# A hand-built first stage with its loops written out: magnitudes from scaled exponentials, tables in two halves, another drain order, and V's scale found earlier

## The chip, the cores and the metric

One core of a Trainium2 chip runs one program on five engines that go their own ways and meet at semaphores: PE (TensorE, matmuls), DVE (VectorE), ACT (ScalarE), POOL (GpSimd) and SP (SyncE, which here only issues DMAs). The metric is the device time of one execution in microseconds; less is better.

## The reference, cut to what matters

```
def _s4d_kernel(log_dt, C, B, inv_A_real, A_imag, L):        # H=128 heads, N=64 modes, L=1024
    dt = jnp.exp(log_dt)
    A = -jnp.exp(inv_A_real) + 1j * A_imag
    dtA = A * dt[:, None]
    Cc = Bc[None, :, :] * (C[..., 0] + 1j * C[..., 1])
    Cc = Cc * (jnp.exp(dtA) - 1.0) / A
    V = jnp.exp(dtA[:, :, None] * ell)                        # ell = 0..1023
    return 2.0 * jnp.einsum('chn,hnl->chl', Cc, V).real       # C is the input x, (16, 128, 64, 2)

h = _L0_tok_ref(...)                                          # the call above
h = h + _L0_attn_ref(_layernorm(h), Wq, bq, Wk, bk, Wv, bv, Wo, bo)      # 32 heads, causal
h = h + _L0_ffn_ref(_layernorm(h), gate, up, down: 4-bit levels plus low-rank parts, silu)
```

Only the first line of `h` and the layer norm behind it belong to the stage that is changed. Attention and the feed-forward part are the same in both kernels.

## The kernel before, in words

The program is one first stage, `ssm_and_norm`, a barrier, and then `layer` with everything else. The first stage makes `h` (written to `h0_tokens`) and its layer norm, split into two 16-bit parts `x_hi` and `x_lo` for the matmuls behind it. It works on all five engines at once.

**The front.** A power exp(dtA·l) is split over l = 128·i + 16·j1 + j0, so three short tables (8 + 8 + 16 = 32 entries for each head, 128 heads: 128 partitions by 4096) give all powers by products. The partitions are the 64 modes twice, for real and imaginary part. DVE makes dt and A (L305 to L318), then the phases (L324 to L332), which ACT turns into sines (L259 to L263). POOL makes the exponents of the magnitudes (L197) and ACT takes the exponential of all 4096 in one instruction (L253). DVE makes the coefficient of each mode by some fifty small operations on 128x128 (L333 to L384). Then the tables are multiplied by the magnitudes, `tab2` on POOL (L200) and `tab1` on DVE (L387), and DVE turns the coefficients into `a1` and `a2` (L391 to L397).

**The units.** Heads are taken 8 at a time, 16 units. For each unit:

- POOL makes the first half of `v` (L208) and the factors `w` (L211, L214), DVE the rest of `w` (L405), the second half of `v` (L407, into `v_second`) and their sum (L410);
- PE multiplies, `product` (L228, 16 fp32 matmuls that stand as 32 in the trace), ACT copies the result out, `columns` (L269, tile `n_xt`);
- PE transposes it, `to_tokens` (L235), ACT copies that out, `tokens` (L279, `n_tok`), and SP writes it to DRAM (L185);
- DVE takes mean and variance (L414 to L417), ACT the root (L273), DVE the inverse (L421, L422), ACT normalises (L283);
- PE transposes back, `to_features` (L242), ACT writes the high part (L287), DVE the low part (L426).

Every engine runs a fixed order of these steps, written by hand with a lag in units for each step. In visit k PE does `to_features(k-5)`, `product(k-1)`, `to_tokens(k-2)`; ACT does `columns(k-2)`, the root of k-4, `tokens(k-3)`, `normalise(k-4)`, `high(k-5)`; DVE does the inverse of k-4, the factors of k, the mean of k-3, `low(k-5)`. Visits in the middle are turns of a hardware loop (`Fori`) with two units each, the first three and the last three pairs are written out. Most tiles have two buffers, `n_pt`, `n_pn` and `v_second` have one.

**V's scale.** While this runs, the first group of V's weights is in SBUF (`wv_raw`). Its largest value over all partitions sets a power of two: `find_big` on DVE (L530), `exchange` by two DMAs through DRAM on SP (L517, L519), `find_scale` on DVE (L536 to L540), then `first.high` on ACT (L545) and `first.low` on DVE (L550) split it. `find_big` and `find_scale` stand in the last visits of DVE, the exchange behind SP's loop.

Of the kernel before, what the change touches and what calls it, by code (L numbers as in the profile page):

```python
# [11 lines left out]
ALU = mybir.AluOpType  # L12
# [3 lines left out]
P = 128  # L16
# [65 lines left out]
LAG = 6  # L82


def ssm_and_norm(nc, ssm, cr, ci, h0_dram, xn_hi, xn_lo, ident, w_first, wv_first, b_first, first, rooms):
# [9 lines left out]
    with ExitStack() as st:  # L95
        sb = rooms.filler("v2", "small")

        def sem(name):
# [50 lines left out]
        def channels(n, s, start=0, end=UH):  # L149
            return bass.ds((n * 2 + s) * UH + start, end - start)  # L150

        def run(eng, stages, chain=None, marks=0, tail=lambda n: None):

            def iterations(n, known):
                for b in two:
                    for lag, work in stages:
                        d = b - lag
                        if not known or 0 <= 2 * n + d < UNITS:
                            work(n + d // 2, d % 2)

            for n in range(LAG // 2):
                iterations(n, True)
            before = chain.count if chain else 0
            with eng.Fori(0, VIS - LAG // 2) as n:
                if chain:
                    chain.loop(n, marks)
                iterations(n + LAG // 2, False)
            if chain:
                chain.end(VIS - LAG // 2, marks, before)
            for n in range(VIS, VIS + LAG // 2):  # L170
                iterations(n, True)
                tail(n - VIS)

        @block.sync
        def _(sp):
            sp.dma_start(par[:], ssm).then_inc(s_in, 16)
            sp.dma_start(cre[:], cr).then_inc(s_c, 16)
            sp.dma_start(cim[:], ci).then_inc(s_c, 16)
            sp.dma_start(first.bias[:], b_first).then_inc(first.s_bias, 16)
            sp.dma_start(first.raw_v[:], wv_first).then_inc(first.s_raw_v, 16)  # L180
            sp.dma_start(first.raw[:], w_first).then_inc(first.s_raw, 16)
            with sp.Fori(0, VIS) as n:
                for s in two:
                    sp.wait_ge(s_tok[s], n + 2)
                    sp.dma_start(h0_dram[:, channels(n, s), :], tok[s][:]).then_inc(s_out[s], 16)  # L185
            first.exchange(sp, 0)
            for s in two:
                sp.wait_ge(s_out[s], 16 * VIS + 16)

        @block.gpsimd  # L190
        def _(pool):
# [9 lines left out]
            pool.wait_ge(s_tab2, 1)  # L201
            pool.wait_ge(s_tab1, 1)
            pool.wait_ge(s_c, 32)

            def factors(n, s):

                pool.wait_ge(s_mm[s], n + 1)
                nc.gpsimd.tensor_tensor(four(v[s], TJ), bc(tab1[:, channels(n, s), TI:2 * TI], TJ, 3),  # L208
                                        bc(tab1[:, channels(n, s), 2 * TI:TAB], TI, 2), ALU.mult).then_inc(s_v1[s], 1)
                pool.wait_ge(s_a, 2)  # L210
                nc.gpsimd.tensor_tensor(four(w[s][0], C), bc(a1[:, channels(n, s), :], C, 3),  # L211
                                        bc(cre[:, channels(n, s), :], KT, 2), ALU.mult)
# [1647 lines left out]
```

## Time and profile before

| | us |
|---|---|
| median of 3 runs | 2087.96 |
| lowest, highest | 2087.77, 2090.44 |
| the profiled execution, time | 2088.66 |
| the profiled execution, span | 2086.7 |

The span runs from the first to the last instruction. PE is busy for 1896.5 us of it (91%), DVE for 1163.6 (56%), ACT for 612.7 (29%), POOL for 618.0 (30%). The chain of work that ended last is PE's for 73% of the span, DVE's for 8%. In forty slices of the span PE is busy for nine tenths or more from the eleventh slice to the end; in the first four slices (52 us each) it is busy for 0, 3, 7 and 7 tenths, and DVE for 8, 9, 9 and 8. The granted clock of PE is printed beside the busy times of a stretch as a share of its full 2.4 GHz; its other level is 1.2 GHz.

A row of the timeline is: start, duration (both us), engine, line, operation, tile written <- tiles read, shapes; in brackets how long the engine had been idle, and who ended that. Rows of a line give in ns the least, the median and the greatest duration, then the first and last start in us. SPq is SP's queue of DMA issues.

### The profile page before, as it was taken

Reading aid. Unit: us, or ns where it says so; the run is one execution under the profiler, and the core shown is the slowest. Engines: PE = TensorE matmul, PEld = TensorE weight load, DVE = VectorE, ACT = ScalarE, POOL = GpSimd, SP = SyncE. Lnnn points to the kernel's source line nnn. Section 1 sums busy time; section 2 is a strip of 40 time slices with the busy share of each in tenths; the row PEclk is TensorE's granted clock in tenths of the full one; section 3 lists DMA queues with packets and bytes.
Section 4 is the critical chain, followed back from the end, with each engine's and each line's share of the span. In section 5 each row is a group of like instructions: output and inputs, shape, how many; then the busy total and the mean of one; then the engine's idle time right before and its main releaser. Section 6 shows DMA issues by size and latency. Waiting matters only on the chain.

```text
span 2086.7 us, 31307 instructions
## 1 busy us (share of the span) xinstructions
PE 1896.5 (91%) x13212; PEld 1029.0 (49%) x13212; DVE 1163.6 (56%) x1476; ACT 612.7 (29%) x869; POOL 618.0 (30%) x261
## 2 busy tenths in 40 slices
PE   0377699999999898878999999999999999999999
PEld 0367576666656554444554444444444444444444
DVE  8998547777777778855644544444444444210111
ACT  2154324334333334421112333333333333200000
POOL 2675013343333334433310322232232232011101
PEclk9998799999999999999999999999999999999999
DMA  2022211111132112135441321322322232533441
GB/s 90 10 71 60 65 35 33 39 39 35 29 94 72 27 36 60 57 104 194 154 147 61 119 94 62 101 91 61 101 91 77 85 101 72 195 120 116 142 142 41
DMA packets 99812, 173.32 MB, mean 83 GB/s; under 512 B 13984, under 2 KB 75168, under 8 KB 91744
## 3 DMA queue, kind: packets, MB, share of 16 engines
q1 hardware_dynamic: 99680, 171.41, 25.7%
q8 instruction: 102, 1.67, 0.3%
q14 instruction: 30, 0.25, 0.0%
HBM read 114.22 MB, written 56.11 MB: 82 GB/s over the span
## 4 chain that ended last, share of the span: by engine, by line
PE 73%; DVE 8%; POOL 2%; issue 2%; ACT 2%; DMA 1%; SPq 1%; ACTq 0%; DVEq 0%
PE acc L1194 14%; PE acc L1123 14%; PE acc L1124 14%; PE ps_p L930 3%; PE ps_p L931 3%; PE ps_p L932 3%; PE acc L1044 3%; PE acc L1045 3%; PE acc L1046 3%; PE ps_t L957 2%; PE ps_p L946 2%; PE ps_p L948 2%; PE ps_p L947 2%; DVE prob L1464 2%; PE ps_l L1139 2%
## 5 line engine op out<-in xcount | busy, mean ns | idle before, releaser
L1123 PE MATMUL acc<-x_hi,q_f 128*128 128x512 f16 x1376 | 522.0, 379 | 0.0
L1124 PE MATMUL acc<-x_lo,q_f 128*128 128x512 f16 x1376 | 521.5, 379 | 0.0
L1194 PE MATMUL acc<-down_levels,hid_parts 128*128 128x512 f16 x1376 | 300.1, 379 | 0.0
L890 POOL TENSOR_TENSOR prob<-prob,mx 128x1024 f32<-128x1024 f32 x64 | 121.4, 1897 | 421.9 <-DVE mx L1471 421.9
L1123 PEld LDWEIGHTS acc<-x_hi,q_f 128*128 128x128 f16 x1376 | 134.5, 98 | 174.8 <-issue 17.8
L899 POOL TENSOR_SCALAR q_f<-q_raw 128x2048 f16<-128x2048 int32 x22 | 121.1, 5504 | 316.3 <-PE acc L1124 315.4
L1194 PEld LDWEIGHTS acc<-down_levels,hid_parts 128*128 128x128 f16 x1376 | 133.2, 98 | 163.1 <-issue 5.0
L1124 PEld LDWEIGHTS acc<-x_lo,q_f 128*128 128x128 f16 x1376 | 134.7, 98 | 156.9
L930 PE MATMUL ps_p<-x_hi,w_qk 128*128 128x512 f16 x512 | 196.8, 384 | 0.0
L931 PE MATMUL ps_p<-x_lo,w_qk 128*128 128x512 f16 x512 | 196.0, 383 | 0.0
L932 PE MATMUL ps_p<-x_hi,w_qk 128*128 128x512 f16 x512 | 195.7, 382 | 0.0
L1749 DVE TENSOR_TENSOR y<-acc,down_scale 128x1024 f32<-128x1024 f32 (+1 forms) x17 | 19.8, 1162 | 252.3 <-PE acc L1194 252.3
L228 PE MATMUL ssm_ps<-phase,magnitude 128*128 128x128 f32 x512 | 73.7, 313 | 87.9 <-DVE magnitude L410 87.9
L1699 DVE SCALAR_TENSOR_TENSOR up<-acc,gu_scale,low_term 128x512 f32<-128x512 f32 x84 | 63.0, 750 | 154.7 <-PE acc L1124 154.7
L946 PE MATMUL ps_p<-w_v,x_hi 128*128 128x256 f16 x512 | 140.6, 275 | 9.0 <-PEq L674 8.8
L948 PE MATMUL ps_p<-w_v,x_lo 128*128 128x256 f16 x512 | 140.6, 275 | 0.0
L947 PE MATMUL ps_p<-w_v,x_hi 128*128 128x256 f16 x512 | 140.6, 275 | 0.0
L1375 ACT ACTIVATE low_term<-ps_l,g_b_back 128x512 f32<-128x512 f32 x168 | 106.0, 682 | 115.6 <-PE ps_l L1139 115.6
L1392 ACT ACTIVATE hidden<-up 128x512 f16<-128x512 f32 (+1 forms) x88 | 55.4, 629 | 287.3 <-DVE up L1708 287.3
L893 POOL TENSOR_TENSOR prob<-prob,sm 128x1024 f32<-128x1024 f32 x64 | 120.4, 1897 | 57.0 <-DVE sm L1478 57.0
L1689 DVE SCALAR_TENSOR_TENSOR gate<-acc,gu_scale,low_term 128x512 f32<-128x512 f32 x84 | 63.0, 751 | 117.9 <-ACT low_term L1375 117.9
L1253 ACT ACTIVATE pth<-ps_t 128x512 f16<-128x512 f32 x128 | 76.0, 594 | 161.0 <-PE ps_t L957 161.0
(284 smaller groups left out, 3081.5 us busy)
## 6 DMA issues: line engine op xcount, KB each, us to landing
q_raw<-in_gu_q SPq DMA_DIRECT2D x22, 1024.0 KB, 7.1
hidden_parts<-hidden SPq DMA_DIRECT2D x42, 512.0 KB, 3.5
hid_parts<-hidden_parts SPq DMA_DIRECT2D x15, 1376.0 KB, 6.7
down_raw<-in_down_q SPq DMA_DIRECT2D x22, 512.0 KB, 5.1
w_raw<-in_w_qk SPq DMA_DIRECT2D x8, 1024.0 KB, 4.8
h_tokens<-n_tok SPq DMA_DIRECT2D x16, 512.0 KB, 3.8
o_parts<-ot SPq DMA_DIRECT2D x32, 256.0 KB, 2.3
wv_raw<-in_w_o SPq DMA_DIRECT2D x8, 1024.0 KB, 4.8
```

The costliest lines, as they stand in the source:

```text
L890: nc.gpsimd.tensor_tensor(prob[s % 2][p][:], prob[s % 2][p][:], bc(mx[p][:], H, 2), ALU.subtract).then_inc(s_sub[p], 1)
L893: nc.gpsimd.tensor_tensor(prob[s % 2][p][:], prob[s % 2][p][:], bc(sm[p][:], H, 2), ALU.mult).then_inc(s_prob[p], 1)
L899: nc.gpsimd.tensor_scalar(q16[i % 2][:], qraw[:], Q_ZERO, None, ALU.subtract).then_inc(s_q, 1)
L930: nc.tensor.matmul(out[:], w[:, j % 2, m, 0, at], xn_hi[:, k, tok], start=(k == 0), stop=False)
L931: nc.tensor.matmul(out[:], w[:, j % 2, m, 0, at], xn_lo[:, k, tok], start=False, stop=False)
L932: last = nc.tensor.matmul(out[:], w[:, j % 2, m, 1, at], xn_hi[:, k, tok], start=False, stop=(k == KT - 1))
L946: nc.tensor.matmul(out, xn_hi[:, k, tok], wv[:, g % 2, 0, at], start=(k == 0), stop=False)
L947: nc.tensor.matmul(out, xn_hi[:, k, tok], wv[:, g % 2, 1, at], start=False, stop=False)
L948: last = nc.tensor.matmul(out, xn_lo[:, k, tok], wv[:, g % 2, 0, at], start=False, stop=(k == KT - 1))
L1123: nc.tensor.matmul(acc[u % 2][:, m, :], lev, x2_hi[:, k, tok], start=(k == 0), stop=False)
L1124: last = nc.tensor.matmul(acc[u % 2][:, m, :], lev, x2_lo[:, k, tok], start=False, stop=(k == KT - 1))
L1194: last = nc.tensor.matmul(acc[n % 2][:, b, :], parts[n % 3][:, at], levels[:, i, b * CH:(b + 1) * CH], start=(i == 0 and part == 0), stop= ...
```

## The change

In both kernels the steps compute the same things on the same tiles. What differs:

- **Magnitudes.** POOL's product L197 and ACT's one exponential of 4096 are gone. ACT writes the 32 entries one by one: 32 instructions of 128x128, each the exponential of `t[2]` with the step as its scale.
- **Halves.** Phases, sines, table products and `a1`/`a2` are done for heads 0 to 63 and then for 64 to 127. Both table products are now DVE's (POOL's L200 is gone). The second half's `a1`/`a2` steps are spread over DVE's visits 1 to 3.
- **Loops.** The hardware loops are gone, every unit is written out, and semaphores count units; the increments by SP ahead of the stage (`start_free`, 18 of them) are gone with them.
- **Order.** PE in visit k: `product(k)`, `to_tokens(k-1)`, `to_features(k-3)`. ACT: `columns(k)`, `normalise(k-2)`, `tokens(k-1)`, `high(k-3)`, `deviation(k-1)`. DVE: `inverse(k-2)`, the rest of `w` and second half of `v` of unit k+1, `mean(k-1)`, and only then the sum `power(k+1)`, then `low(k-3)`.
- **V's scale.** `find_big` stands in DVE's visit 7, `find_scale` in visit 12, SP's exchange behind the output of unit 11, and the two parts of `first.high` and `first.low` in the last visits.

DVE, one visit in the middle, as its instructions stand before (inverse of unit k-4, factors of k, mean of k-3, low part of k-5):

```order
L421 RECIPROCAL n_rs1_122<-n_std1_120 128x1 [waits a_std1]
L422 SCALAR_TENSOR_TENSOR n_rs1_122<-n_mv1_118,n_rs1_122 128x1 [waits a_dve]
L405 TENSOR_TENSOR phase_106<-a2_109,c_im_85 128x640 [waits a_mm1]
L407 TENSOR_TENSOR magnitude_107<-w_v_52 128x1024 [waits a_v0]
L410 TENSOR_TENSOR magnitude_107<-magnitude_107 128x1024 [waits a_v11,a_dve]
L414 BN_STATS n_stats0_115<-n_tok0_113 128x6 [waits a_tok0]
L415 BN_STATS n_stats0_115<-n_tok0_113 128x6
L417 BN_AGGR n_mv0_117<-n_stats0_115 128x2 [waits a_dve]
L426 TENSOR_TENSOR x_lo_64<-n_pn,x_hi_63 128x128x8 [waits a_hi0]
```

The same engine and place after the change (`power`, which completes `v`, is now L435, and `mean` is L439 to L441):

```order
L447 RECIPROCAL n_rs0_121<-n_std0_119 128x1 [waits a_nrm,a_std]
L448 SCALAR_TENSOR_TENSOR n_rs0_121<-n_mv0_117,n_rs0_121 128x1 [waits a_dve]
L425 TENSOR_TENSOR phase_106<-a2_109,c_im_85 128x640 [waits a_mm]
L431 TENSOR_TENSOR magnitude_107<-w_v_52 128x1024 [waits a_v]
L439 BN_STATS n_stats1_116<-n_tok1_114 128x6 [waits a_tok,a_dve]
L440 BN_STATS n_stats1_116<-n_tok1_114 128x6
L441 BN_AGGR n_mv1_118<-n_stats1_116 128x2 [waits a_dve]
L435 TENSOR_TENSOR magnitude_107<-magnitude_107 128x1024 [waits a_v1]
L452 TENSOR_TENSOR x_lo_64<-n_pn,x_hi_63 128x128x8 [waits a_hi]
```

The sum that completes `v` moved from ahead of the mean to behind it, and the unit whose mean it follows is now two behind the unit of the sum, where it was three.

ACT, one visit in the middle before (`columns`, root, `tokens`, `normalise`, `high`):

```order
L269 ACTIVATE n_xt1_112<-ssm_ps1 128x1024 [waits a_tr1,a_mm1]
L273 ACTIVATE n_std1_120<-n_mv1_118,n_eps_123 128x1 [waits a_mv1]
L279 ACTIVATE n_tok0_113<-n_pt 128x1024 [waits a_out0,a_nrm0,a_tr0]
L283 ACTIVATE magnitude_107<-n_tok1_114,n_rs1_122 128x1024 [waits a_rs1,a_trn1]
L287 ACTIVATE x_hi_63<-n_pn 128x128x8 [waits a_trn0]
```

and after (`columns`, `normalise`, `tokens`, `high`, root):

```order
L256 ACTIVATE n_xt1_112<-ssm_ps1 128x1024 [waits a_tr,a_mm]
L274 ACTIVATE magnitude_107<-n_tok1_114,n_rs1_122 128x1024 [waits a_trn,a_tab,a_rs]
L263 ACTIVATE n_tok0_113<-n_pt 128x1024 [waits a_mean,a_out0,a_tr]
L278 ACTIVATE x_hi_63<-n_pn 128x128x8 [waits a_trn]
L267 ACTIVATE n_std0_119<-n_mv0_117,n_eps_123 128x1 [waits a_mean]
```

`normalise` moved from behind `tokens` to ahead of it, the root to the end.

The core of the diff:

```diff
-LAG = 6
+STEPS_OF = [P * k for k in range(TI)] + [TJ * k for k in range(TI)] + list(range(TJ))
+HALF_H = H // 2
...
-            with sp.Fori(0, VIS) as n:
-                for s in two:
-                    sp.wait_ge(s_tok[s], n + 2)
-                    sp.dma_start(h0_dram[:, channels(n, s), :], tok[s][:]).then_inc(s_out[s], 16)
-            first.exchange(sp, 0)
+            for u in range(UNITS):
+                sp.wait_ge(s_tok, u + 1)
+                sp.dma_start(h0_dram[:, channels(u), :], tok[u % 2][:]).then_inc(s_out[u % 2], 16)
+                if u == UNITS - 5:
+                    first.exchange(sp, 0)
...
-            pool.wait_ge(s_const, 3 + 15)
-            pool.wait_ge(s_z, 1)
-            nc.gpsimd.tensor_tensor(mag[:], bc(t[2][:], TAB, 2), bc(steps[:], H, 1), ALU.mult).then_inc(s_decay, 1)
-            pool.wait_ge(s_trig, 5)
-            pool.wait_ge(s_mag, 1)
-            nc.gpsimd.tensor_tensor(tab2, tab2, mag[:], ALU.mult).then_inc(s_tab2, 1)
...
-            run(pool, [(0, factors)])
+            for u in range(UNITS):
+                s, ch, cut = u % 2, channels(u), channels(u, 0, CUT)
+                pool.wait_ge(s_tab, 1 + 2 * u // UNITS)
+                pool.wait_ge(s_trig, 2)
+                if u >= 2:
+                    pool.wait_ge(s_mm, u - 1)
+                nc.gpsimd.tensor_tensor(four(v[s], TJ), bc(tab1[:, ch, TI:2 * TI], TJ, 3), bc(tab1[:, ch, 2 * TI:TAB], TI, 2),
+                                        ALU.mult).then_inc(s_v1, 1)
+                pool.wait_ge(s_a, 2 if u < UNITS // 2 else 4)
+                nc.gpsimd.tensor_tensor(four(w[s][0], C), bc(a1[:, ch, :], C, 3), bc(cre[:, ch, :], KT, 2), ALU.mult)
+                nc.gpsimd.tensor_tensor(four(w[s][1], C)[:, 0:CUT], bc(a2[:, cut, :], C, 3), bc(cim[:, cut, :], KT, 2),
+                                        ALU.mult).then_inc(s_wp, 1)
...
-            run(pe, [(5, to_features), (1, product), (2, to_tokens)])
+            for k in range(UNITS + 3):
+                if each(0, k):
+                    product(k)
+                if each(1, k):
+                    to_tokens(k - 1)
+                if each(3, k):
+                    to_features(k - 3)
...
-            act.wait_ge(s_decay, 1)
-            nc.scalar.activation(mag[:], mag[:], ACT.Exp).then_inc(s_mag, 1)
+            for k, step in enumerate(STEPS_OF):
+                last = nc.scalar.activation(mag[:, :, k], t[2][:], ACT.Exp, scale=float(step))
+            last.then_inc(s_mag, 1)
...
-            run(act, [(2, columns), (4, deviation), (3, tokens), (4, normalise), (5, high)])
-            first.high(nc, act, 0, 0)
-            first.high(nc, act, 0, 1)
+            for k in two:
+                hs = heads(k)
+                act.wait_ge(s_phase, k + 1)
+                nc.scalar.activation(tab1[:, hs, 0:2 * TI], tab1[:, hs, 0:2 * TI], ACT.Sin, scale=-TWO_PI, bias=quarter[:])
...
+            for k in range(UNITS + 3):
+                if each(0, k):
+                    columns(k)
+                if each(2, k):
+                    normalise(k - 2)
+                if each(1, k):
+                    tokens(k - 1)
+                if each(3, k):
+                    high(k - 3)
+                if each(1, k):
+                    deviation(k - 1)
+                if k in (UNITS - 1, UNITS):
+                    act.wait_ge(s_v, UNITS)
+                    first.high(nc, act, 0, k - UNITS + 1)
...
-            chain.mark(nc.vector.tensor_copy(t[6][:], t[3][:]))
-            chain.after(tt(phase[:], bc(t[3][:], TAB, 2), bc(steps[:], H, 1), ALU.mult))
-            chain.after(ts(tab1, phase[:], MAGIC, MAGIC, ALU.add, ALU.subtract))
-            tt(phase[:], phase[:], tab1, ALU.subtract).then_inc(s_phase, 1)
...
+            for k in two:
+                hs = heads(k)
+                chain.after(tt(phase[:, hs, :], bc(t[3][:, hs], TAB, 2), bc(steps[:], HALF_H, 1), ALU.mult))
+                chain.after(ts(tab1[:, hs, :], phase[:, hs, :], MAGIC, MAGIC, ALU.add, ALU.subtract))
+                chain.after(tt(phase[:, hs, :], phase[:, hs, :], tab1[:, hs, :], ALU.subtract))
...
+            def tables(k):
+                hs = heads(k)
+                dve.wait_ge(s_trig, k + 1)
+                chain.mark(tt(tab1[:, hs, :], tab1[:, hs, :], mag[:, hs, :], ALU.mult))
+                tt(tab2[:, hs, :], tab2[:, hs, :], mag[:, hs, :], ALU.mult).then_inc(s_tab, 1)
...
-            tt(tab1, tab1, mag[:], ALU.mult).then_inc(s_tab1, 1)
-            dve.wait_ge(s_tab1, 1)
-            dve.wait_ge(s_tab2, 1)
...
+            tables(0)
+            dve.wait_ge(s_tab, 1)
+            for part in range(3):
+                rotations(0, part)
+            tables(1)
...
+                    dve.wait_ge(s_mm, u - 1)
+                tt(four(w[s][1], C)[:, CUT:UH], bc(a2[:, hs, :], C, 3), bc(cim[:, hs, :], KT, 2), ALU.mult).then_inc(s_wd, 1)
...
+            def power(u):
+                dve.wait_ge(s_v1, u + 1)
+                tt(v[u % 2], v[u % 2], v_second, ALU.add).then_inc(s_v, 1)
...
+            for k in range(-1, UNITS + 3):
+                if each(2, k):
+                    inverse(k - 2)
+                if each(-1, k):
+                    second_factor(k + 1)
+                    second_power(k + 1)
+                if each(1, k):
+                    mean(k - 1)
+                if each(-1, k):
+                    power(k + 1)
+                if 1 <= k < 4:
+                    rotations(1, k - 1)
+                if k == UNITS - 9:
                     first.find_tops(nc, dve, chain)
                     first.find_big(nc, dve, chain, 0)
-                if n == 1:
+                if k == UNITS - 4:
                     first.find_scale(nc, dve, chain, 0)
-
-            run(dve, [(4, inverse), (0, factors), (3, moments), (5, low)], chain, 2 * 4, weights)
-            first.low(nc, dve, 0, 0)
-            first.low(nc, dve, 0, 1)
+                if each(3, k):
+                    low(k - 3)
+                if k in (UNITS, UNITS + 1):
+                    first.low(nc, dve, 0, k - UNITS)
```

## Rows read from the trace of the kernel before

**Rows 1.** The page, its first line.

```profile
span 2086.7 us, 31307 instructions
```

**Rows 2.** Timeline of the front, 14 to 67 us, columns as told above.

```profile
14.58 7.08 POOL L197 TENSOR_TENSOR magnitude<-ssm_t,table_steps 128x4096 f32<-128x4096 f32 x1 [9.41 <-DVE ssm_t L318]
...
14.60 11.34 DVE L324 TENSOR_TENSOR phase<-ssm_t,table_steps 128x4096 f32<-128x4096 f32 x1
...
14.68 0.29 ACT L251 ACTIVATE ssm_t<-ssm_t 128x128 f32<-128x128 f32 x1
...
25.98 2.29 DVE L325 TENSOR_SCALAR w_qk<-phase 128x4096 f32<-128x4096 f32 x1
...
28.30 4.43 DVE L326 TENSOR_TENSOR phase<-phase,w_qk 128x4096 f32<-128x4096 f32 x1
...
32.77 2.29 DVE L330 SCALAR_TENSOR_TENSOR w_qk<-phase 128x2048 f32<-128x2048 f32 x1
...
39.50 0.22 DVE L333 TENSOR_SCALAR ssm_t<-ssm_t 128x128 f32<-128x128 f32 x1
...
47.71 8.89 DVE L363 TENSOR_TENSOR ssm_t<-ssm_t,ssm_t 128x128 f32<-128x128 f32 x1
...
61.69 4.42 DVE L387 TENSOR_TENSOR w_qk<-w_qk,magnitude 128x4096 f32<-128x4096 f32 x1
...
66.15 1.23 DVE L391 TENSOR_TENSOR a<-ssm_t,w_qk 128x1024 f32<-128x1024 f32 x1
```

**Rows 3.** Lines of the units, over the whole span: ns, first and last start.

```profile
L208 POOL TENSOR_TENSOR magnitude<-w_qk x16: 1922/2868/2905, 66.2 to 193.2; 128x1024 f32 x10, 128x1024 f32<-128x1024 f32 x6
...
L405 DVE TENSOR_TENSOR phase<-a,c_im x16: 809/812/2547, 75.2 to 195.1; 128x640 f32 x10, 128x640 f32<-128x640 f32 x6
...
L407 DVE TENSOR_TENSOR magnitude<-w_v x16: 1211/2399/2949, 75.9 to 195.8; 128x1024 f32 x10, 128x1024 f32<-128x1024 f32 x6
...
L269 ACT ACTIVATE n_xt<-ssm_ps x16: 999/1025/1028, 86.6 to 209.9; 128x1024 f32<-128x1024 f32 x16
...
L283 ACT ACTIVATE n_nrm<-n_tok,n_rs x8: 1240/1241/1247, 105.8 to 218.8; 128x1024 f32<-128x1024 f32 x8
...
L279 ACT ACTIVATE n_tok<-n_pt x16: 1004/1006/1025, 92.6 to 214.1; 128x1024 f32<-128x1024 f32 x16
```

**Rows 4.** Timeline of PE: the first product, and three steps at 152 to 164 us.

```profile
80.70 5.91 PE L228 MATMUL ssm_ps<-phase,magnitude 128*128 128x128 f32 x32 [80.70 <-DVE magnitude L410]
...
152.19 1.07 PE L242 MATMUL n_pn<-ident,magnitude 128*128 128x128 f32 x8 [3.75 <-DVE x_lo L426]
...
153.09 5.37 PE L228 MATMUL ssm_ps<-phase,magnitude 128*128 128x128 f32 x32
...
160.50 3.74 PE L228 MATMUL ssm_ps<-phase,magnitude 128*128 128x128 f32 x32
```

**Rows 5.** Timeline of DVE at 116 us: mean and variance, and what follows.

```profile
116.67 0.69 DVE L414 BATCH_NORM_STATS2 n_stats<-n_tok 128x6 f32<-128x512 f32 x1
...
118.22 1.17 DVE L426 TENSOR_TENSOR x_lo<-n_pn,x_hi 128x1024 f16<-128x1024 f32 x1
```

**Rows 6.** Timeline from the last product to the first work of the next stage.

```profile
215.20 0.17 DVE L524 SCALAR_TENSOR_TENSOR b_top<-b_qkv 128x24 f32<-128x24 f32 x1
...
218.38 0.34 SPq L517 DMA_DIRECT2D wv_bigs<-wv_big  x1
...
226.45 0.33 SPq L519 DMA_DIRECT2D wv_all<-wv_bigs  x1
...
230.75 0.29 DVE L536 TENSOR_REDUCE wv_pow<-wv_all 128x1 f32<-128x128 f32 x1 [4.09 <-DMA wv_all<-wv_bigs]
...
232.04 1.22 DVE L426 TENSOR_TENSOR x_lo<-n_pn,x_hi 128x1024 f16<-128x1024 f32 x1
...
233.34 2.48 DVE L550 SCALAR_TENSOR_TENSOR w_v<-wv_raw,wv_scale,w_v 128x1024 f16<-128x1024 f32 x2
...
237.55 0.37 PE L946 MATMUL ps_p<-w_v,x_hi 128*128 128x256 f16 x1 [8.80 <-PEq L674]
```

More of the change, by code:

```diff
@@ L147, in four, with channels, heads, each @@
             return room.rearrange("p (h a b) -> p h a b", h=UH, b=n)
[L149 to L172, printed above, removed]
+        def channels(u, start=0, end=UH):
+            return slice(u * UH + start, u * UH + end)
+        def heads(k):
+            return slice(k * HALF_H, (k + 1) * HALF_H)
+        def each(lag, k):
+            return 0 <= k - lag < UNITS
         @block.sync
@@ L275, in tokens @@
-            def tokens(n, s):
-                act.wait_ge(s_tr[s], n + 2)
-                act.wait_ge(s_nrm[s], n + 1)
-                act.wait_ge(s_out[s], n * 16 + 16)
-                nc.scalar.activation(tok[s][:].rearrange("p (i j) -> p i j", j=P), pt[:], ACT.Copy).then_inc(s_tok[s], 1)
-            def normalise(n, s):
-                apart(act, s_passed, (s_rs[s], n + 1), (s_trn[s], n + 1))
-                nc.scalar.activation(nrm[s], tok[s][:], ACT.Identity, scale=rs[s][:, 0:1], bias=rs[s][:, 1:2]).then_inc(s_nrm[s], 1)
@@ new lines, in columns, with tokens @@
+            def columns(u):
+                act.wait_ge(s_mm, u + 1)
+                if u >= 2:
+                    act.wait_ge(s_tr, u - 1)
+                nc.scalar.activation(xt[u % 2][:], ps[u % 2][:].rearrange("p h m -> p m h"), ACT.Copy).then_inc(s_ev, 1)
+            def tokens(u):
+                act.wait_ge(s_tr, u + 1)
+                if u >= 2:
+                    act.wait_ge(s_out[u % 2], 16 * (u // 2))
+                    act.wait_ge(s_mean, u - 1)
+                nc.scalar.activation(tok[u % 2][:].rearrange("p (i j) -> p i j", j=P), pt[:], ACT.Copy).then_inc(s_tok, 1)
@@ L333, in _ @@
+            chain.after(nc.vector.tensor_copy(t[6][:], t[3][:]))
             ts(t[8][:], t[6][:], MAGIC, MAGIC, ALU.add, ALU.subtract).then_inc(s_turn0, 1)
@@ new lines, in second_power, with mean @@
+            def second_power(u):
+                ch = channels(u)
+                if u:
+                    dve.wait_ge(s_v, u)
+                chain.after(tt(four(v_second, TJ), bc(tab2[:, ch, TI:2 * TI], TJ, 3), bc(tab2[:, ch, 2 * TI:TAB], TI, 2), ALU.mult))
+            def power(u):
+                dve.wait_ge(s_v1, u + 1)
+                tt(v[u % 2], v[u % 2], v_second, ALU.add).then_inc(s_v, 1)
+            def mean(u):
+                dve.wait_ge(s_tok, u + 1)
+                chain.mark(nc.vector.bn_stats(stats[u % 2][:, 0, :], tok[u % 2][:, 0:512]))
+                chain.after(nc.vector.bn_stats(stats[u % 2][:, 1, :], tok[u % 2][:, 512:D]))
+                nc.vector.bn_aggr(mv[u % 2][:], stats[u % 2][:].rearrange("p a b -> p (a b)")).then_inc(s_mean, 1)
@@ new lines, in inverse, with low @@
+            def inverse(u):
+                dve.wait_ge(s_std, u + 1)
+                if u >= 2:
+                    dve.wait_ge(s_nrm, u - 1)
+                chain.after(nc.vector.reciprocal(rs[u % 2][:, 0:1], std[u % 2][:]))
+                stt(rs[u % 2][:, 1:2], mv[u % 2][:, 0:1], -1.0, rs[u % 2][:, 0:1], ALU.mult, ALU.mult).then_inc(s_rs, 1)
+            def low(u):
+                dve.wait_ge(s_hi, u + 1)
+                tt(xn_lo[:].rearrange("p k (c h) -> p k c h", h=H)[:, :, :, channels(u)], pn[:].rearrange("p k (c h) -> p k c h", h=UH),
+                   xn_hi[:].rearrange("p k (c h) -> p k c h", h=H)[:, :, :, channels(u)], ALU.subtract).then_inc(s_lo, 1)
```

192 lines of the change are left out of this document (82 added, 110 removed).

## The prediction

> **What bounds the kernel now.** I read four views. The page gives the span of 2086.7 us [rows 1]; the profiled execution took 2088.66, 2.0 more, and the median of the runs is 0.7 below it. The timeline of the last steps shows that the next stage starts at 237.55 us with PE's first matmul of V [rows 6], behind a barrier that all engines pass. Nothing of that stage starts earlier and its work is unchanged, so whatever the first stage gains or loses is the result. The stage has three parts. The front ends with the first product at 80.70 [rows 4]. The units run from the end of product 0 to that of product 15; ACT's copy L269 starts within 0.1 us of each, at 86.6 and at 209.9 [rows 3], so 15 units take 123.3 us, 8.2 each. The tail is 209.9 to 237.55, 27.7 us. In the front DVE is the engine that is waited for, and POOL holds it up twice. In the units DVE and POOL take turns: one DVE product of 1024 takes 1.21 us at best and 2.40 in the median, POOL's 1.92 and 2.87 [rows 3]. PE waits for them between its products, 3.75 us at 152 us [rows 4].
>
> **Front, until the first product.** DVE's L324 and POOL's L197 start together and take 11.34 and 7.08 us; the like product L326 takes 4.43 alone [rows 2]. With L197 gone, DVE has 11.34 - 4.43 = 6.9 us back. L363, a 128x128 operation, takes 8.89 us behind POOL's L200, and its neighbours 0.3: with L200 gone, 8.6 back. Cutting the phases in halves adds nothing but six starts, under 0.3 us. So DVE reaches the table products at 61.69 - 6.9 - 8.6 = 46.2.
>
> ACT's 32 exponentials, at most 0.29 each [rows 2], last from about 14.1 to 23.4. They cost nothing, as DVE asks for the magnitudes at 46.2; cover is 22 us. The sines of the second half can start at about 14.6 + 18 = 32.6. The whole set fits before between 39.50 and 47.71, 8.2 us, so the half is done by 37: hidden too, by the coefficient chain of DVE.
>
> From 46.2 DVE has the first half of both tables (4.4, as much as L387), six steps of 512 for `a1` and `a2` (0.65 each by L391's 1.23, 3.9), the second half of the tables (4.4) and the three steps of unit 0 (0.81 + 1.21 + 1.21 = 3.2). That is 15.9 us, ending at 62.1 were POOL silent. It isn't: as soon as the first half of the tables stands, POOL starts on units 0 and 1, 1.92 + 1.92 + 0.7 = 4.6 us each. If all of it falls on DVE, v(0) stands at 71.3. Before, the first unit took from 75.2 to 80.70, 5.5 us for DVE's 3.2: 2.3 lost over three instructions. Eleven instructions lie in the contended stretch now, so 8.4 lost: 70.5, and I take that; ends 62.1 and 71.3. The rows say that a DVE operation with two operands waits for POOL's to end. The Trainium skill (SBUF — State Buffer, Who interferes with whom) calls it an exclusive lock on a port pair that DVE and GpSimd share, with the loser blocked for the whole instruction; by that rule alone the front would end at 71.3 instead, 0.8 us later, and the trace agrees with it in L324 and L363.
>
> Product 0 takes 5.91 from idle [rows 4], end at 76.4 instead of 86.6: **-10.2**.
>
> **The units.** Here the orders of three engines close a ring. Follow it in the rows of order. DVE's `power(k+1)` completes v(k+1), without which `product(k+1)` can't start. In DVE's order `mean(k-1)` stands right ahead of it, and waits for `tokens(k-1)` on ACT. ACT has `columns(k)` and `normalise(k-2)` ahead of that, and `columns(k)` waits for `product(k)`. So from the end of one product to the start of the next nothing overlaps: columns 1.02, normalise 1.24, tokens 1.01 [rows 3], mean and variance until the next DVE operation 118.22 - 116.67 = 1.55 [rows 5], the sum 1.21: 6.0 us. Before, the sum stood ahead of a mean three units back, and no such ring existed. PE's two transposes (1.07 each, so 2.1) and POOL's next unit (4.6 from the end of the product) run beside these 6.0. POOL ends just as the sum would start; at most 0.1 for each unit.
>
> The product itself took 5.37 or 3.74 [rows 4]. In this trace the product that followed 3.75 us of idle PE, with only a set of transposes between, took 5.37, and the one with PE busy shortly before took 3.74. In the ring PE idles 6.0 - 2.1 = 3.9 us in every unit. So I take 5.37 for all, and 3.74 and 5.91 as the ends. One unit then lasts **11.4 us**, against 8.2.
>
> Starting: product 1 follows product 0 at once (3.74, end 80.2). For product 2, columns, tokens (no normalise yet), mean and sum take 4.8, and POOL, with two units in a row to make, about 1 more; 5.37 behind it, end at 91.4. From product 0 to 2: 15.0. Thirteen further units: 148.2.
>
> DVE has room in the ring: of 11.4 us it spends 2.8 on mean and sum, 3.6 on low part, inverse and the two factor steps, so 5.0 are free. The three spread steps of the second half (1.3 each) and `find_big` (215.20 to 218.38, 3.2 us [rows 6]) fit and cost nothing. `find_scale` doesn't. SP's exchange starts behind the output of unit 11, 3.7 us after the end of product 12. The first DMA took 226.45 - 218.38 = 8.1, the second until DVE went on 4.3, `find_scale` 232.04 - 230.75 = 1.3: DVE is through at +17.4. Queued behind it on DVE are low(9) 1.2, inverse(11) 0.4; then ACT's normalise(11) and tokens(12) 2.3; then mean and sum 2.8: v(14) stands at +24.0 instead of 11.4 + 6.0 = 17.4. Cost **6.6 us** once; 0 if the exchange were to land within DVE's free time, about 10 if the 512 KB output ahead of it in the queue delays it by its own transfer.
>
> From product 0 to 15: 15.0 + 148.2 + 6.6 = 169.8 against 123.3: **+46.5**.
>
> **The tail.** It has fewer units in flight (3 behind the product, before 4), and V's exchange, which there kept DVE from 218.4 to 232.0, is out of it. Counted from product 15's end: tokens(14) 3.3, mean 4.8, low(12) 6.0, inverse 6.5, normalise(14) 7.7, tokens(15) 8.7, mean(15) 10.3, low(13) 11.5, first.low 12.7, inverse(15) 13.1, normalise(15) 14.3, high(14) 15.3, low(14) 16.5, first.low 17.8, beside it transposes and high(15) 18.7, low(15) 19.9. From DVE's last work (233.34 + 2.48 = 235.82) to 237.55 were 1.7. Sum 21.6 against 27.7: **-6.1**.
>
> **Sum.** -10.2 + 46.5 - 6.1 = +30.2, so 2118.9 for an execution like the profiled one, and 2118 for the median.
>
> **The rivals.**
>
> - *PE stays at its faster clock* (3.74 for each product). For it: the same 2.4 GHz held through some shorter idle stretches. Against: 5.37 behind 3.75 us. Saves 13 x 1.63 = 21: **2097**. With half of the products so: **2108**.
> - *The ring does not bind*, and units keep a cadence of 8.2. It would be so if tokens(k-1) stood ready before product(k) ends, which the written order denies. Then 15.0 + 13 x 8.2 + 6.6 = 128.2, +4.9, with the front and the tail -11.4: **2077**, faster. It decides at a unit of about 9.1 us: below that the gains of front and tail win.
> - *The second-half work or the exchange costs more than I count*: the exchange at its upper end (+3.4), products at 5.91 (+7): **2128**.
> - *The front gives nothing* (POOL's units, which now start earlier, eat all that its two big products gave back): +10, also **2128**. Against: 9.2 us of POOL's work in all are in its way.
>
> **Chances.** Forecast with its neighbours at 2112 to 2124: 0.50. Half or all products fast, 2096 to 2112: 0.27. The two dear cases, 2124 to 2133: 0.13. Faster, about 2077: 0.07. In between, near no change: 0.03. A measurement of this kernel tells about 0.2% (4 us) from no change. So faster 0.07, within 0.2% 0.03, slower 0.90. The range 2096 to 2131 leaves out 0.07 + 0.03 and about 0.05 at the top and gaps.
>
> **What would show it.** In the changed profile: first product near 70.5, without any DVE row of 8 us ahead of it. Product starts 11.4 apart, each right behind DVE's L435, and L435 right behind L441; DVE idle ahead of L439, released by ACT's L263, for 3 to 5 us in each unit; ACT's L263 back to back with L274 and L256. One DVE wait for the DMA of `wv_all` of about 10 us behind unit 11. Next stage's first matmul near 268. I am wrong if DVE is busy without gaps in the units, or if the products lie 8 us apart.

## The result, and the profile after

| | before | after |
|---|---|---|
| median, us (4 runs each) | 2087.86 | 2125.14 |
| lowest, highest | 2087.72, 2090.44 | 2123.59, 2127.61 |
| the profiled execution | 2088.66 | 2124.87 |

The ratio is 1.0177, with a 95% interval from 1.0159 to 1.0194: slower, and by the medians by 37.3 us. Forecast were 2118 us in a range of 2096 to 2131.

The page of the changed kernel, its span and the group of the product; the last column of the group is PE's idle time ahead of it and who ended it:

```profile
span 2123.1 us, 31041 instructions
...
L204 PE MATMUL ssm_ps<-phase,magnitude 128*128 128x128 f32 x512 | 92.9, 366 | 129.6 <-DVE magnitude L435 129.6
```

Of 2123.1 us, 36.4 more than [rows 1], PE idles 129.6 ahead of the first stage's products (70.4 of it ahead of the very first), and always until DVE's L435, the sum that completes `v`. The next stage's first matmul (first row below of the last group) starts at 275.22 where [rows 6] has 237.55: +37.7. From there to the end of the span it is 1847.9 us, before 1849.2. So all of the loss lies in the first stage.

**The front.** Its timeline, to hold against [rows 2] (`L393` and `L392` are the table products, one half of the heads each):

```profile
13.89 7.25 ACT L237 ACTIVATE magnitude<-ssm_t 128x128 f32<-128x128 f32 x32
...
13.93 2.29 DVE L328 TENSOR_TENSOR phase<-ssm_t,table_steps 128x2048 f32<-128x2048 f32 x1
...
46.67 2.29 DVE L392 TENSOR_TENSOR w_qk<-w_qk,magnitude 128x2048 f32<-128x2048 f32 x1
...
57.08 4.03 POOL L188 TENSOR_TENSOR phase<-a,c_re 128x1024 f32<-128x1024 f32 x1 [3.41 <-DVE a L409]
...
64.56 2.94 DVE L431 TENSOR_TENSOR magnitude<-w_v 128x1024 f32<-128x1024 f32 x1
...
67.52 2.83 DVE L435 TENSOR_TENSOR magnitude<-magnitude 128x1024 f32<-128x1024 f32 x1
...
70.41 9.02 PE L204 MATMUL ssm_ps<-phase,magnitude 128*128 128x128 f32 x64 [70.41 <-DVE magnitude L435]
```

The phase steps are short without POOL beside them, no row of 8 us is left, and the tables start at 46.67 (46.2 was forecast, 61.69 it was). ACT's 32 exponentials take 7.25 us together and end at 21.1, 25 us before they are asked for. From 51 us on POOL's units overlap DVE's steps, and from 57 us on they hold them: 2.94 and 2.83 for what takes 1.22 alone. The first product starts at 70.41, ten us before that of [rows 4].

**The units.** One turn of the ring in the changed kernel and the start of the next, ACT, DVE and PE in order of time:

```profile
150.88 1.03 ACT L256 ACTIVATE n_xt<-ssm_ps 128x1024 f32<-128x1024 f32 x1 [6.36 <-PE ssm_ps L204]
...
151.81 1.23 ACT L274 ACTIVATE magnitude<-n_tok,n_rs 128x1024 f32<-128x1024 f32 x1
...
152.94 1.01 ACT L263 ACTIVATE n_tok<-n_pt 128x1024 f32<-128x1024 f32 x1
...
154.05 0.69 DVE L439 BATCH_NORM_STATS2 n_stats<-n_tok 128x6 f32<-128x512 f32 x1 [5.46 <-ACT n_tok L263]
...
155.37 0.21 DVE L441 BATCH_NORM_AGGREGATE n_mv<-n_stats 128x2 f32<-128x12 f32 x1
...
155.50 1.21 DVE L435 TENSOR_TENSOR magnitude<-magnitude 128x1024 f32<-128x1024 f32 x1
```

```profile
156.76 6.58 PE L204 MATMUL ssm_ps<-phase,magnitude 128*128 128x128 f32 x32 [4.17 <-DVE magnitude L435]
...
163.38 1.02 ACT L256 ACTIVATE n_xt<-ssm_ps 128x1024 f32<-128x1024 f32 x1 [7.47 <-PE ssm_ps L204]
```

The ring of the prediction is there step by step: product, columns L256, normalise L274, tokens L263, mean L439 to L441 after 5.46 us of idle DVE, sum L435, product. From the end of a product to the start of the next are 5.9 us, in all units from 4 to 13 but one with 6.2 (PE's bracket says 4.17, as its transposes lie in the gap). Before, the units took 8.2 us [rows 3]; here 10 units, from 97.63 to 217.16, took 119.5: 11.95 each.

The products come in two lengths, in turn, 5.47 and 6.57. The granted clock goes with it. Columns are: stretch, us, PE busy (instructions), granted clock, DMA share, GB/s.

```profile
145.40:146.40 1.00, 1.00 (x5) 0.54 0.36 139
148.40:149.40 1.00, 1.00 (x9) 0.75 0.00 0
154.40:155.40 1.00, 0.00 (x0) 1.00 0.25 66
155.40:156.40 1.00, 0.00 (x0) 0.66 1.05 193
161.40:162.40 1.00, 1.00 (x6) 0.50 0.00 0
162.40:163.40 1.00, 1.00 (x10) 0.92 0.00 0
168.40:169.40 1.00, 0.14 (x1) 0.99 0.91 258
```

Ahead of a long product the clock falls to one half (1.2 GHz) while PE idles, about 1 us before the product starts (155.7 for 156.76), and comes back to full (2.4 GHz) 5.7 us into it, at about 162.5. Ahead of a short one it stays full through the gap and falls only within 0.3 us of the product's start: the product at 145.38 has 0.54 in its first microsecond, and the stretch that holds the start of the one at 169.26 still has 0.99. It is back 3.5 us into the product, at about 148.9. In stretches of 0.2 us all of products 4 to 13 follow one of these two courses, in turn.

**The exchange and the tail.**

```profile
214.93 0.59 SPq L554 DMA_DIRECT2D wv_bigs<-wv_big  x1
...
223.53 0.33 SPq L556 DMA_DIRECT2D wv_all<-wv_bigs  x1
...
227.89 0.29 DVE L573 TENSOR_REDUCE wv_pow<-wv_all 128x1 f32<-128x128 f32 x1 [10.79 <-DMA wv_all<-wv_bigs]
...
235.61 6.42 PE L204 MATMUL ssm_ps<-phase,magnitude 128*128 128x128 f32 x32 [3.14 <-DVE magnitude L435]
...
253.39 1.03 ACT L256 ACTIVATE n_xt<-ssm_ps 128x1024 f32<-128x1024 f32 x1 [6.30 <-PE ssm_ps L204]
...
275.22 0.37 PE L983 MATMUL ps_p<-w_v,x_hi 128*128 128x256 f16 x1 [4.03 <-PEq L711]
```

DVE waits 10.79 us for `wv_all`. Product 14 starts 18.5 us behind product 13 (217.16) and not 11.4, 7.1 lost. ACT copies product 15 out at 253.39; the next stage follows 21.8 us later, where it was 27.7.

### The profile page after: what moved, and what is told of

Its sections match the earlier page's. It is cut to its first block, busy times and chain, and to the rows that moved or that the text cites. A ratio compares the mean times of both kernels' runs of the same rounds, so it can differ in the third digit from the quotient of the medians.

```text
span 2123.1 us, 31041 instructions
## 1 busy us (share of the span) xinstructions
PE 1913.0 (90%) x13212; PEld 1046.4 (49%) x13212; DVE 1126.7 (53%) x1491; ACT 616.5 (29%) x905; POOL 584.8 (28%) x259
## 4 chain that ended last, share of the span: by engine, by line
PE 70%; DVE 8%; POOL 2%; issue 2%; DMA 2%; ACT 2%; SPq 1%; ACTq 0%; DVEq 0%
PE acc L1231 14%; PE acc L1160 14%; PE acc L1161 14%; PE ps_p L967 3%; PE acc L1081 3%; PE acc L1082 2%; PE acc L1083 2%; PE ps_p L968 2%; PE ps_p L969 2%; PE ps_t L994 2%; PE ps_p L983 2%; PE ps_p L985 2%; PE ps_p L984 2%; DVE prob L1501 2%; PE ps_l L1176 2%
## 5 line engine op out<-in xcount | busy, mean ns | idle before, releaser
L204 PE MATMUL ssm_ps<-phase,magnitude 128*128 128x128 f32 x512 | 92.9, 366 | 129.6 <-DVE magnitude L435 129.6
L204 PEld LDWEIGHTS ssm_ps<-phase,magnitude 128*128 128x128 f32 x512 | 90.1, 278 | 133.1 <-DVE magnitude L435 133.1
```

The lines of the kernel that those rows point to most:

```text
L204: last = nc.tensor.matmul(ps[s][:, h, :], v[s][:, cols], w[s][k][:, cols], start=(k == 0), stop=(k == 1))
```

## Experiments

All are edits of the changed kernel, timed beside the kernel before on the same chip (its medians 2088.5 to 2088.8, against 2087.86 in the table above, so a difference to 2125.14 is good to about 1 us).

**1. The sum ahead of the mean.** The one exchange of two steps on DVE that the prediction made responsible, undone:

```diff
-                if each(1, k):
-                    mean(k - 1)
                 if each(-1, k):
                     power(k + 1)
+                if each(1, k):
+                    mean(k - 1)
```

> The changed kernel with one pair of steps exchanged on DVE: power(k+1) stands ahead of mean(k-1) again. Ring theory: products no longer wait for the mean, so they come at the pace of DVE and POOL, about 8.2 us apart instead of 11.9; 13 units x 3.7 = 48 us less, the wait for the exchange stays: about 2077 us (2068 to 2087), DVE's L435 released by POOL or by nothing. Rival theory (the shorter lags between all steps, three units in flight instead of four, slow the units): products stay 11 to 12.5 us apart, 2120 to 2128 us.

Measured: 2091.79 us (10 runs, 2088.51 to 2094.58), ratio to before 1.0014 [1.0004, 1.0025]. It takes 33.4 of the 37.3 us away. The order of these two steps is the cause of nearly all of the loss. But with units of 8.2 back, 2077 (2068 to 2087) was expected, and this is 15 us above it. Products and the DVE steps between them, in this kernel:

```profile
114.80 5.32 PE L204 MATMUL ssm_ps<-phase,magnitude 128*128 128x128 f32 x32 [4.76 <-DVE magnitude L435]
...
121.70 3.74 PE L204 MATMUL ssm_ps<-phase,magnitude 128*128 128x128 f32 x32
...
123.25 0.69 DVE L439 BATCH_NORM_STATS2 n_stats<-n_tok 128x6 f32<-128x512 f32 x1 [2.58 <-ACT n_tok L263]
...
125.97 1.58 DVE L448 SCALAR_TENSOR_TENSOR n_rs<-n_mv,n_rs 128x1 f32<-128x1 f32 x1
...
128.21 2.95 DVE L431 TENSOR_TENSOR magnitude<-w_v 128x1024 f32<-128x1024 f32 x1
...
131.19 1.74 DVE L435 TENSOR_TENSOR magnitude<-magnitude 128x1024 f32<-128x1024 f32 x1
...
132.99 6.41 PE L204 MATMUL ssm_ps<-phase,magnitude 128*128 128x128 f32 x32 [5.80 <-DVE magnitude L435]
```

Products now come in pairs, here 6.9 and 11.3 us apart; over ten units (94.76 to 192.95) 9.8 a unit. Inside a pair nothing waits for DVE. Ahead of the next pair DVE first waits 2.58 us for ACT's tokens, which stand behind the product, columns and normalise; then it goes from L439 at 123.25 to the end of L435 at 132.93 without a gap, and is slow where POOL works beside it: 2.95 for 1.22, 1.74 for 1.23, and 1.58 for an operation on one column (L448) that takes 0.16 elsewhere. Such slow rows stand in the kernel before as well [rows 3]; why the units took 8.2 us there and 9.8 here no run takes apart. Added to it are `find_big`, behind which a product comes late (154.09, 13.1 us behind the one ahead of it), and the exchange (8.5 us wait of DVE).

**2. Tokens ahead of normalise.** Shortens the ring by one ACT step and leaves it closed. (The added wait is for a count that stands by then; it keeps the buffer of `n_tok` safe.)

```diff
                     act.wait_ge(s_mean, u - 1)
+                    act.wait_ge(s_nrm, u - 1)
...
-                if each(2, k):
-                    normalise(k - 2)
                 if each(1, k):
                     tokens(k - 1)
+                if each(2, k):
+                    normalise(k - 2)
```

> The changed kernel with tokens(k-1) ahead of normalise(k-2) on ACT, and a wait that is long satisfied. Ring theory: 1.1 us less between the end of a product and the start of the next, in 13 or 14 units, so 15 us less, 2110 us; if the products' own times change with PE's clock, 2103 to 2116. Rival theory (ACT is idle for more than half of a unit and does not set the pace): 2125 us, products 11.9 apart.

Measured: 2109.99 us (4 runs, 2105.42 to 2111.37), ratio 1.0094 [1.0073, 1.0114]. So 15.2 us less, the size that was expected, but its parts are others. From the tokens to the product:

```profile
144.63 1.02 ACT L264 ACTIVATE n_tok<-n_pt 128x1024 f32<-128x1024 f32 x1
...
145.73 1.92 POOL L188 TENSOR_TENSOR phase<-a,c_re 128x1024 f32<-128x1024 f32 x1
...
147.19 1.54 DVE L436 TENSOR_TENSOR magnitude<-magnitude 128x1024 f32<-128x1024 f32 x1
...
148.79 5.18 PE L204 MATMUL ssm_ps<-phase,magnitude 128*128 128x128 f32 x32 [3.38 <-DVE magnitude L436]
```

PE's idle time ahead of a product falls only from 4.17 to 3.38, 0.8 for a step of 1.13: POOL's L188 still runs when DVE's sum starts, and the sum takes 1.54 for 1.21. Ten units (96.18 to 203.42) take 107.2 us, 10.7 each, 12.3 less than in the changed kernel. Nearly half of that, 5.7 us, is the products, which take 5.2 to 5.5 us now in all but one of these units, where long ones of 6.6 came in turn before; the rest is the gaps.

**3. The exchange three units earlier.**

```diff
-                if u == UNITS - 5:
+                if u == UNITS - 8:
                     first.exchange(sp, 0)
```

> The changed kernel with SP's exchange behind the output of unit 8 instead of unit 11; find_scale stays in DVE's visit 12. If DVE's wait for the DMA (10.8 us idle in the trace) costs what it delays v(14), product 14 comes 6.9 us sooner and the time is 2118 us. Rival theory (the wait only takes the place of a wait for tokens): 2125 us.

Measured: 2117.62 us (4 runs, 2116.58 to 2119.79), ratio 1.0140 [1.0123, 1.0157]: 7.5 us less, for the 6.6 of the prediction and the 7.1 of the trace. Product 14 keeps the pace (11.4 us behind product 13), and DVE's wait for `wv_all` is gone:

```profile
215.90 5.45 PE L204 MATMUL ssm_ps<-phase,magnitude 128*128 128x128 f32 x32 [4.17 <-DVE magnitude L435]
...
227.26 6.54 PE L204 MATMUL ssm_ps<-phase,magnitude 128*128 128x128 f32 x32 [4.17 <-DVE magnitude L435]
```

**4. PE kept busy.** In visits 3 to 14, behind `to_features`, 14 matmuls of the identity with itself into a free PSUM buffer. They add work and no result.

```diff
+            def keep_busy(k):
+                pe.wait_ge(s_ev, k)
+                for i in range(14):
+                    nc.tensor.matmul(ps[(k + 1) % 2][:, i % UH, :], ident[:], ident[:], start=True, stop=True)
...
+                if 3 <= k < UNITS - 1:
+                    keep_busy(k)
```

> The changed kernel with 14 matmuls of the identity into the free PSUM buffer behind to_features in visits 3 to 14, which fill about 3.2 of PE's 4.2 idle us; their result is overwritten by the next product. Clock theory: products 4 to 15 take 3.74 us instead of 5.4 to 6.6, 2.3 less each, 12 of them: 27 us less, 2098 us, granted clock 1.00 in the units. Rival theory (the products are long for another reason, such as where their operands come from): products stay at 5.4 to 6.6, 2125 us or some us more where the added matmuls run into the next product.

Measured: 2103.57 us (4 runs, 2103.38 to 2106.57), ratio 1.0074 [1.0056, 1.0091]. Work that nobody needs makes it 21.6 us faster. The products take 3.84 us from product 4 on (the last but one 3.74), mostly 9.76 apart; the granted clock from 96 to 190 us, here and in the changed kernel (columns: stretch, us, busy us of PE, PEld, DVE, ACT, POOL, each with its instructions, granted clock, DMA share, GB/s):

```profile
96.00:190.00 94.00, 80.24 (x686) 78.53 (x687) 62.55 (x92) 38.66 (x46) 43.68 (x27) 0.98 0.20 54
```

```profile
96.00:190.00 94.00, 62.17 (x384) 60.27 (x384) 50.27 (x80) 32.93 (x39) 34.98 (x24) 0.78 0.17 45
```

The ring is unchanged: 9.76 less 3.84 is 5.9. Products 4 to 15 are 25.9 us shorter together, near the 27 of the forecast. Most of what is missing to 2098 lies in two places. `find_big` (147.71 to 150.79) moves DVE's next steps beside POOL's: L455 takes 1.69 for 0.16 and L438 2.95 for 1.22, and product 9 comes 12.3 us behind product 8, 2.5 late. And the exchange stalls product 14 by 9.1 us, where it was 7.1.

**5. The front undone.** POOL's product and one exponential over all heads, in place of the 32:

```diff
+            pool.wait_ge(s_const, 3 + 15)
+            pool.wait_ge(s_re, 1)
+            nc.gpsimd.tensor_tensor(mag[:], bc(t[2][:], TAB, 2), bc(steps[:], H, 1), ALU.mult).then_inc(s_sq, 1)
...
-            for k, step in enumerate(STEPS_OF):
-                last = nc.scalar.activation(mag[:, :, k], t[2][:], ACT.Exp, scale=float(step))
-            last.then_inc(s_mag, 1)
+            act.wait_ge(s_sq, 1)
+            nc.scalar.activation(mag[:], mag[:], ACT.Exp).then_inc(s_mag, 1)
```

> The changed kernel with one part of the front undone: POOL's product and ScalarE's one exponential over all heads are back, in place of the 32 small exponentials. Theory, the front's gain is real and reaches the end one for one: the exponentials of before were ready at 45.56 for tables that could start at 46.7, so the 4.43 us exponential and the 8 us product must come ahead of the tables. POOL's product can start where the distances are ready, near 14; if VectorE's phase work beside it is delayed as in [rows 2], the tables start some 5 to 8 us later than 46.67 and the first product near 76 to 78 instead of 70.41, so 2125.1 + 5.5 to 7.5 = 2131 to 2133 us. Rival, the front is hidden behind the arrival of other work and gives nothing: 2125 us and a first product at 70.4.

Measured: 2132.93 us (4 runs, 2132.03 to 2135.30), ratio 1.0217 [1.0201, 1.0233]: 7.8 us slower than the changed kernel.

```profile
13.22 7.08 POOL L180 TENSOR_TENSOR magnitude<-ssm_t,table_steps 128x4096 f32<-128x4096 f32 x1 [8.91 <-DVE ssm_t L320]
...
13.30 7.08 DVE L322 TENSOR_SCALAR ssm_t<-ssm_t 128x128 f32<-128x128 f32 x1
...
20.33 3.62 ACT L240 ACTIVATE magnitude<-magnitude 128x4096 f32<-128x4096 f32 x1 [6.73 <-POOL magnitude L180]
...
76.91 9.35 PE L207 MATMUL ssm_ps<-phase,magnitude 128*128 128x128 f32 x64 [76.91 <-DVE magnitude L437]
```

A DVE operation of 128x128, which takes 0.23 us elsewhere, starts 0.08 behind POOL's and ends with it: both 7.08. The tables start at 53.18 for 46.67 and the first product 6.5 us later; the next stage's first matmul comes at 282.25 for 275.22, 7.0 later. So this part of the front's gain is real and reaches the end. The way was another than expected. The exponential costs nothing: it is ready at 23.95, 29 us before the tables, and all of the 6.5 us is DVE held by POOL. The expectation also has figures that are not those of the kernel before, where the exponential took 3.62 us and was ready at 25.32 (not 4.43 and 45.56) and POOL's product took 7.08. The other part of the front, POOL's L200 gone, was not undone by itself.

**6. Sum first and exchange early together.** Both edits as above.

> Two edits together, both off the changed kernel: the sum of the next unit ahead of the mean of the last one on VectorE, and the exchange of V's scale behind unit 8 instead of unit 11. Sum first alone took 2091.8 us and the early exchange alone took 7.5 us off. If the two costs lie one behind the other (the stall ahead of product 14 is at 202.85 in the trace of sum first, 8.52 us long), they add: 2091.8 - 7.5 = 2084.3 us (2082 to 2088), which is just faster than the kernel before at 2088.7. Rival: in the faster units the wait for the exchange is covered by the slack between products, and nothing more goes than the noise: 2091 us.

Measured: 2083.23 us (8 runs, 2081.82 to 2085.01), ratio 0.9974 [0.9964, 0.9985]. The two costs add, and with both gone the kernel is faster than before, by 0.26%.

**7. Tokens first as well.** Edits 1, 2 and 3 together.

> Sum first and early exchange as in the run before it, and ScalarE's tokens ahead of its normalise as well. If a ring through the tokens still sets the distance of the products after the sum went first, 1.1 us a unit go again: 2084 - 13 x 1.1 = 2070 us. Theory: with the sum first, no product hangs on the tokens of the unit ahead of it any more; VectorE's and ScalarE's own orders set the pace, so the tokens' place gives 0 to 0.3 us a unit: 2080 to 2085 us.

Measured: 2077.17 us (5 runs, 2076.47 to 2080.02), ratio 0.9951 [0.9937, 0.9965]. Between the two forecasts: 6 us off, where they had 0 to 4 and 14. PE, the first product of one pair to that of the next:

```profile
169.21 5.26 PE L204 MATMUL ssm_ps<-phase,magnitude 128*128 128x128 f32 x32 [4.99 <-DVE magnitude L436]
...
186.52 6.77 PE L204 MATMUL ssm_ps<-phase,magnitude 128*128 128x128 f32 x32 [4.99 <-DVE magnitude L436]
```

A pair takes 17.3 us, against 19.5 in the same place of experiments 1 and 6. The tokens still count there: DVE's mean waits for them ahead of the next inverse and the factors, 1.41 us at 176.48, where it was 2.58 in experiment 1.

**8. And PE kept busy.** Edits 1 to 4 together.

> The kernel of the run before it with 14 idle matmuls a unit on TensorE, which brought the products of the changed kernel from 5.47 and 6.57 us to 3.84. They take 3.3 us a unit themselves. If the length of the products is part of the distance of 9.9 us a unit that sum first left (products 3.74 and 5.3 to 6.7 us in turn), each unit gives 1 to 2 us: 13 x 1.5 = 20 us off, near 2062 us. Rival: TensorE was waited for in the short gap only, the idle matmuls stand in the way of the waiting transposes, and it gets 5 to 20 us slower, 2090 to 2105 us.

Measured: 2077.87 us (4 runs, 2077.63 to 2078.76), ratio 0.9949 [0.9934, 0.9965]: no change against 7. Neither theory had it. All products but a few take 3.74, but they stand 8.44 us apart with no idle time of PE between: the extra matmuls (2.96) now are the bound themselves, just where the pairs had been.

**9. Six extra matmuls instead of 14.**

```diff
-                for i in range(14):
+                for i in range(6):
```

> The kernel of the run with 14 idle matmuls a unit, but with 6. There the products stood 8.44 us apart with no idle time of TensorE: 3.74 for the product, 0.87 and 0.87 for the two sets of transposes, 2.96 for the idle matmuls. With 6 of them TensorE needs 3.74 + 1.74 + 1.27 = 6.75 us a unit, and VectorE some 7.0 (its rows of one unit there, 8.44 less the wait of 1.79 for the tokens, plus 0.3 of small gaps). Theory, TensorE's own work was the bound of that run and six idle matmuls still keep it at the short product: products about 7.2 us apart, 10 units x 1.2 = 12 us off, 2066 us (2062 to 2071). Rival, with gaps in its work the products take 5.2 to 5.5 us in turn again: the pairs of 17.4 us of the run with no idle matmuls come back, 2077 us.

Measured: 2075.40 us (6 runs, 2073.52 to 2079.07), ratio 0.9939 [0.9925, 0.9953]. The fastest of all, though not told apart from 7 for certain, and 9 us above the 2066 that was expected. Where it runs evenly, products stand 7.5 us apart, for the 7.2 expected. In three places they don't; two of them are here:

```profile
131.88 3.84 PE L204 MATMUL ssm_ps<-phase,magnitude 128*128 128x128 f32 x32 [0.59 <-DVE magnitude L443]
...
139.42 3.84 PE L204 MATMUL ssm_ps<-phase,magnitude 128*128 128x128 f32 x32 [0.61 <-DVE magnitude L443]
...
152.82 4.39 PE L204 MATMUL ssm_ps<-phase,magnitude 128*128 128x128 f32 x32
...
179.72 2.83 DVE L443 TENSOR_TENSOR magnitude<-magnitude 128x1024 f32<-128x1024 f32 x1
...
182.61 3.84 PE L204 MATMUL ssm_ps<-phase,magnitude 128*128 128x128 f32 x32 [0.60 <-DVE magnitude L443]
...
183.91 0.23 DVE L581 TENSOR_REDUCE wv_pow<-wv_all 128x1 f32<-128x128 f32 x1
...
187.27 2.96 DVE L439 TENSOR_TENSOR magnitude<-w_v 128x1024 f32<-128x1024 f32 x1
...
190.27 2.83 DVE L443 TENSOR_TENSOR magnitude<-magnitude 128x1024 f32<-128x1024 f32 x1
...
193.15 6.40 PE L204 MATMUL ssm_ps<-phase,magnitude 128*128 128x128 f32 x32 [3.61 <-DVE magnitude L443]
```

From 139.42 to 152.82, 13.4 us, `find_big` stands in DVE's way. From 182.61 to 193.15, 10.5 us, it is `find_scale`: its own 1.2 us (183.91 to 185.15) push L439 of the next unit into POOL's work, where it takes 2.96 in place of 1.22. L443 took 2.83 in the units that run evenly as well (179.72). So 1.2 us more work cost 3.0 between products, and the product behind the gap takes 6.40. Between 104.3 and 115.6 the spread steps of the second half do the same.

## Why the prediction was right, and where its size was off

The sign and the ring hold; the ring was read from the written order and shown by experiment 1. The time came 7 us above the forecast: 2125 lies outside the forecast with its neighbours (2112 to 2124, 0.50) and in the band of the two dear cases (2124 to 2133, 0.13), of which one half came true: products of 5.9.

- **Front.** -10.2 forecast for the end of product 0 (76.4). It ended at 75.9. The steps hold: tables at 46.67 for 46.2, first product at 70.41 for 70.5. That they hold so closely is part luck: the stage started 0.7 us earlier (13.93 for 14.60), and the phases in halves took 18.9 us (13.93 to 32.82), where 18.0 and under 0.3 more were counted. Product 0 took 5.5 for 5.91. Experiment 5 gives POOL's product its price, 6.5 us, for the 6.9 of the text; the 8.6 of L200 rests on the rows alone. The ACT instructions are 0.23 us apart, under the 0.29 taken. The end of 71.3, with all of POOL's work falling on DVE, left out that DVE can be there first: at 57.08 it is POOL's L188 that takes 4.03 for 1.92. The Trainium skill (SBUF — State Buffer, Who interferes with whom) says that whoever starts first holds the shared ports for the whole instruction; the trace agrees both ways, with this row and with DVE's 2.94 and 2.83.
- **Ring.** 6.0 us forecast between products, 5.9 measured, the same steps in the same order; experiment 1 opens it at one step and experiment 2 shortens it by another, and both move the time as a ring through these steps asks. This carried the sign.
- **Length of a product.** The term that was mis-sized. I took 5.37 for all from one row of before [rows 4]; the 13 products behind product 2 took 77.4 us, 5.95 each: +7.6. The row showed a product with a granted clock of 0.68 over its length, so at half clock for about 3.4 us (an estimate from that row). The short products here are such; every second one starts at half clock and stays there for 5.7 us. The upper end of the text, 5.91, was the better value. Experiment 4 shows that it is the idle time and nothing in the product itself.
- **Products 0 to 2.** 15.0 forecast, 15.8 measured; product 2 took 6.54 for 5.37.
- **Exchange.** 6.6 forecast, 7.1 in the trace, 7.5 by experiment 3. DVE's 10.79 us wait for `wv_all` is the 10 of the text.
- **Tail.** 21.6 forecast, 21.8 measured.
- **Sum.** The next stage was forecast near 268 (76.4 + 169.8 + 21.6) and starts at 275.2: 7.4 late, of which 7.6 are the products. The rest of the kernel was 1.3 us shorter, so 2124.9 for 2118.9.
- **Rivals.** "PE fast" came with 3.84 only once PE was filled. "The ring does not bind", 2077, was worked out with units of 8.2 as before; experiment 1 had 2092, as DVE, slowed by POOL and waiting for the tokens once in each pair, sets 9.8 a unit there. It took the tokens' place and the earlier exchange too to get to 2077. "The front gives nothing" is answered by the first product at 70.41 and by experiment 5.

## What to carry to other kernels

In orders written by hand, look for a closed ring, a circle of waits in which a step comes to wait for its own result of the unit before: follow the step that the slowest engine waits for back through every engine's order, and if it comes to that engine's own last result, the steps on the way add up once a unit, however idle the engines are. Here moving one sum of 1.2 us behind a wait cost 33 us. A gap in PE's work cost twice here, once by itself and once by the clock: take a product's length from rows with the same gaps ahead of it, and where these are mixed, keep both lengths.

## What the hardware showed that I had not expected

- The same product with the same 4.17 us of idle PE ahead takes 5.47 and 6.57 us in turn, in products 4 to 13 (one of them has 4.50 ahead and takes 5.36); with 3.38 us ahead (experiment 2) it takes 5.2 to 5.5, with 1.05 (experiment 4) 3.84. The clock falls about 1 us before the long ones and at the start of the short ones; why it does so in turn is open.
- Useless matmuls paid: twelve times some 3 us of them brought 21.6 us, as long as they fitted in the gap (experiment 4), and nothing once they filled it (8).
- A DVE operation on one column next to a POOL operation took 1.58 us in place of 0.16, and one of 128x128 took 7.08 in place of 0.23: in these rows it is not the size that counts but POOL's instruction beside it (1.93 and 7.08 us long).
- A store of 0.5 KB (one number for each partition) took 8.6 us until the next step could go on (214.93 to 223.53), and the 64 KB read back behind it 4.4; in the kernel before they took 8.1 and 4.3.
